# Graph layers of a GNN kernel: GpSimd waits for three landed gathers of the group in front before each group of four

## The reference

```python
def gcn_conv(x, W, b, src, dst, ew, num_nodes):
    h = x @ W
    deg = segment_sum(ew, dst, num_segments=num_nodes)
    dinv = where(deg > 0, rsqrt(deg), 0.0)
    norm = dinv[src] * ew * dinv[dst]
    agg = segment_sum(h[src] * norm[:, None], dst, num_segments=num_nodes)
    return agg + b
...
h = relu(batch_norm(gcn_conv(x, W1, b1, ...)))
h = relu(batch_norm(gcn_conv(h, W2, b2, ...)))
h = batch_norm(gcn_conv(h, W3, b3, ...))
out = layernorm(x + h)
```

## Time and profile before

| | us |
|---|---|
| three runs | 4579.43, 4584.94, 4593.61 |
| median | 4584.94 |
| profiled execution, its own time | 4592.19 |
| its span, first to last instruction | 4590.3 |
| busy: TensorE, VectorE, GpSimd, ScalarE | 2969.0, 2312.5, 2411.3, 1147.0 |
| mean granted TensorE clock, share of full | 0.823 |

### The profile page before, as it was taken

One profiled execution on the slowest core, in us unless ns is written; L12 is line 12 of the kernel. 1 busy time (PEld: TensorE's weight loads), 2 busy tenths in 40 slices (PEclk: granted clock), 3 DMA queues, 4 the chain that ended last, 5 costly groups with the idle time before them and its releaser, 6 DMA issues. The chain is left out here.

```text
span 4590.3 us, 52237 instructions
## 1 busy us (share of the span) xinstructions
PE 2969.0 (65%) x14449; PEld 2143.5 (47%) x14449; DVE 2312.5 (50%) x8186; ACT 1147.0 (25%) x2512; POOL 2411.3 (53%) x2514
## 2 busy tenths in 40 slices
PE   3895666666676666664420666777767776767774
PEld 3774656666666656663200433344433444433342
DVE  3774655655655555553522345533455534455435
ACT  1223556555655555552001200000000000000001
POOL 0002544444466666665577266665466664666662
PEclk9998778777787877776755889988899988999987
DMA  4896555565422322221000455555545545555552
GB/s 110 273 358 232 199 200 210 189 216 191 163 88 80 87 79 81 84 81 48 1 1 0 172 190 174 189 191 184 186 174 190 189 174 179 192 188 176 189 189 61
DMA packets 232026, 706.47 MB, mean 154 GB/s; under 512 B 62326, under 2 KB 111957, under 8 KB 212928
## 3 DMA queue, kind: packets, MB, share of 16 engines
q1 hardware_dynamic: 104252, 447.79, 26.7%
q0 software_dynamic: 93184, 191.21, 14.4%
q10 hardware_dynamic: 34308, 64.13, 4.3%
HBM read 559.66 MB, written 143.28 MB: 153 GB/s over the span
## 5 line engine op out<-in xcount | busy, mean ns | idle before, releaser
L552 POOL DMA_INDIRECT stage<-h_tab,earr x1248 | 1183.3, 948 | 810.8 <-issue 346.5
L527 POOL DMA_INDIRECT arena<-kv_tab,idxr x832 | 796.0, 957 | 970.3 <-ACT idxr L634 405.6
L1013 PE MATMUL bank<-arena,xr 128*128 128x512 f32 (+1 forms) x2058 | 1021.1, 638 | 5.6 <-issue 5.6
L992 PE MATMUL bank<-oh,stage 128*128 128x128 f32 x2496 | 394.3, 308 | 494.0 <-issue 487.8
L992 PEld LDWEIGHTS bank<-oh,stage 128*128 128x128 f32 x2496 | 354.1, 214 | 712.3 <-issue 701.1
L860 PE MATMUL bank<-xr,arena 128*128 x3328 | 494.0, 308 | 236.8 <-DVE arena L1254 146.9
L1572 DVE TENSOR_TENSOR sums<-sums,bank 128x128 f32 x1248 | 351.3, 282 | 568.3 <-remote 398.2
L1013 PEld LDWEIGHTS bank<-arena,xr 128*128 128x128 f32 x2058 | 407.6, 212 | 394.8 <-issue 394.8
L860 PEld LDWEIGHTS bank<-xr,arena 128*128 128x128 f32 x3328 | 456.0, 218 | 259.3 <-issue 258.2
L499 POOL DMA_INDIRECT a_tab<-tot,cell x416 | 416.0, 1000 | 261.2 <-DMA arena<-kv_tab,idxr 151.1
L709 ACT ACTIVATE rs<-mv,epsc 128x49 f32<-128x49 f32 (+1 forms) x6 | 1.9, 316 | 2003.3 <-DVE mv L1611 1692.6
(11 more groups left out here) (224 smaller groups left out, 2739.4 us busy)
## 6 DMA issues: line engine op xcount, KB each, us to landing
arena<-a_tab SPq DMA_DIRECT2D x147, 1792.0 KB
a_tab<-stage SPq DMA_DIRECT2D x49, 1792.0 KB
kv_tab<-stage SPq DMA_DIRECT2D x48, 768.0 KB, 8.5
arena<-key_d ACTq DMA_DIRECT2D x52, 512.0 KB, 7.1
arena<-ew_d ACTq DMA_DIRECT2D x52, 512.0 KB, 10.1
arena<-rel_d SPq DMA_DIRECT2D x52, 512.0 KB
stage<-h_tab,earr POOLq DMA_INDIRECT x1248
arena<-kv_tab,idxr POOLq DMA_INDIRECT x832
```

Source lines behind the costliest of these rows:

```text
L527: G.indirect_dma_start(kv[b % 3][:, t, :], None, kv_tab, bass.IndirectOffsetOnAxis(idxr[:, b % 3, t:t + 1], 0))\
L552: G.indirect_dma_start(gring[:, (q % NG) * GRP + s, :], None, h_tab[l], bass.IndirectOffsetOnAxis(src_i[:, t:t + 1], 0)).then_inc(row_land ...
L992: last = M.matmul(bank[q % NG][:, s * P:(s + 1) * P], gring[:, (q % NG) * GRP + s, :], oh[:, q % NG, s, :], start=True, stop=True)
L1013: mm = M.matmul(o_[:, 0:cw], xr[:, n, :], abuf[B % NBUF][:, n % KB, 0:cw], start=n == 0, stop=n == NT - 1)
```

## The change

Ahead of each group but the first of a layer, GpSimd now also waits until the first three gathers of the group in front have landed, and until the last gather of the group two in front has. For that the landings are told on other semaphores: the first three gathers of a group count on `row_land[q % 4]` (48 a group), the last one on one of two new semaphores `row_last[Q % 2]`. TensorE waits for both ahead of the group's sums.

```diff
+        row_last = [sem(f"row_last{a}") for a in range(2)]
...
                     Q = GQ * l + q
                     if Q >= NG:
                         pool.wait_ge(sum_done, Q - NG + 1)
+                    if q:
+                        pool.wait_ge(row_land[(q - 1) % NG], 48 * ((Q - 1) // NG + 1))
+                    if Q >= 2:
+                        pool.wait_ge(row_last[Q % 2], 16 * (Q // 2))
                     for s in range(GRP):
                         t = q * GRP + s
                         G.indirect_dma_start(gring[:, (q % NG) * GRP + s, :], None, h_tab[l],
-                                             bass.IndirectOffsetOnAxis(src_i[:, t:t + 1], 0)).then_inc(row_land[q % NG], 16)
+                                             bass.IndirectOffsetOnAxis(src_i[:, t:t + 1], 0))\
+                         .then_inc(row_land[q % NG] if s < GRP - 1 else row_last[Q % 2], 16)
...
             def sums(l, q):
                 Q = GQ * l + q
-                pe.wait_ge(row_land[q % NG], 64 * (Q // NG + 1))
+                pe.wait_ge(row_land[q % NG], 48 * (Q // NG + 1))
+                pe.wait_ge(row_last[Q % 2], 16 * (Q // 2 + 1))
```

## The result

The changed kernel takes 4943.9 us (median of 4 runs, 4942.1 to 4954.4) where the kernel before takes 4586.8 (4 runs): a ratio of 1.078, 95% interval 1.077 to 1.080, or 357 us more. The forecast was 4652, with a range up to 4750. The profiled execution has a span of 4940.2 us, against 4590.3 before.

The account below looks back on a forecast made before the run. It took GpSimd's stretch of gathers, with its stops for a full ring, to set each layer's time. 93 + 243 - 269 = +67 us on the median 4585 gave 4652 us, range 4530 to 4750.

Parts of the forecast that it names:

- Step (a): GpSimd's full-ring waits for sum_done ahead of groups go, except each layer's first: 269 us back.
- Step (b): New landing wait ahead of groups in quiet stretches: 0.30 us for each of 309 groups, 93 us (ends 0 and 155).
- Step (c): New landing wait beside block loads: 135 loads at 1.8 us, 243 us lost (ends 135 and 351).
- The rival built on that estimate: Landing wait hidden in quiet stretches, third gather back within 2.5 us: -26 us, 4559 us; chance 0.06.
- on the average half way: Beside block loads, each load meets one third gather, on the average half way: 1.8 us lost per load.
- The fast rival: Block loads fall in with the groups, next third gather meets only their end: -41 us, 4544 us; chance 0.24.
- Ring waits that stay in part: Quiet pauses too short for TensorE's news, half of the 269 us of ring waits stays: +202, 4787 us; chance 0.15.
- One for one: New pauses only stand where GpSimd's ring waits stood: no change, 4585 us; chance 0.09.
- +15 to +130: Whole kernel: range of the sum with the ends of (b) and (c) apart from each other, 4600 to 4715 us.

Follow-up runs that it names:

- second set: Follow-up runs on a chip where the kernel before took 4351.6 us: changed kernel with small loads or 768 KB loads, kernel before with the pause or half rows.
- small loads: Changed kernel, blocks behind the first four load 64 KB instead of 1,792 KB: ratio 1.048 in the second set, later 4606.4 us, 1.0036; kernel before likewise: 4563.7 us.
- the wait on the gather: Changed kernel with the landing wait written first, so the group's first gather carries it itself: 4791.0 us, ratio 1.049.
- timed pieces: Changed kernel, each block loaded in two pieces, each released by the landing of a group's third gather: 4659.6 us, ratio 1.0136.
- the pause: Kernel before plus four GpSimd memsets behind each group's wait for sum_done, no landing waited for: 1.056 in the second set, later 4629.2 us, 1.008.
- half rows: Kernel before, gathers behind the first four groups fetch 64 of 128 rows: ratio 0.995 in the second set, later 4600.8 us, 1.002.
- first, third and fourth set: Follow-up runs, each beside the kernel before, which took 4565.8, 4589.9 and 4591.1 us; the last two on one chip.

## Why the prediction was wrong, point by point

**Step (a), the ring waits: right in kind, 64 us too large.** The pauses for landings took the place of the waits for `sum_done`, as announced: "remote" is gone, the waits for TensorE are 60 us. 205 us came back and not 269. The step counted the 0.30 us of fixed gap ahead of the 113 stopping gathers as stop (290 is 256 without it), and assumed that only a layer's first full ring stays, 21 us, where 53 us net stay (9 of them at the first rings). Its reason, that the pauses together are long enough, held in the result and in three of the four sets; on the chip of the second set there is little to give back.

**Step (b), the quiet stretches: mis-sized, 0.72 instead of 0.30 us a group, 129 us too low.** The landing of a 64 KB gather comes 2.54 us behind its start (median of the small loads in the second set, whose trace has nearly all landings; the attention part's row has 3.00 with the restart in it), and the restart behind the landing takes 0.73 us and not 0.26, because the wait is an instruction of its own. In the earlier trace rows the instruction behind the landing, a scatter, carries its wait itself. The run with the wait on the gather shows 2.74 us from start to restart: for this form the step would have been right (0.27 measured, 0.30 forecast). The order of the instructions would have told it: in the changed kernel the gather carries `sum_done`, and the landing wait stands ahead by itself.

The Trainium skill has, in "DMA: Bandwidth & Descriptors", section "Anatomy of one DMA — SWDGE (gpsimd) path", a price of about 2.0 us plus the bytes over 436 GB/s; for 64 KB that is an estimate of 2.15 us. The traces do not agree, they have 2.54. The rival built on that estimate fell: with the better of the two restarts 2.15 + 0.26 = 2.41 us would have been hidden, and 2.74 were measured.

**Step (c), the loads: mis-sized, 2.5 instead of 1.8 us, 88 us too low.** The number of loads and the mechanism are right: with small loads 342 us go. The step that failed is "on the average half way". Loads don't meet the groups at random. In the timeline above the load is issued at 3707.11 and the third gather starts at 3708.08, close to the worst place. 75 of 139 loads stand like that and cost 3.8 us each, 41 stand about 1 us behind a third gather's start and cost 0.9 us, so they bunch in two places. That they do so because each load follows TensorE's dense steps, once its news is prompt, fits the rows but wasn't tested by itself. The fast rival had seen that the loads would fall into step, and put all of them behind the third landing. The timed pieces show that at that place the price is 0.28 us: the rival's mechanism is real, but most loads were not there.

**The other rivals.** Ring waits that stay in part: 53 us of them, not 135. Its reason, quiet pauses too short for the news, is seen in the run with small loads, where 57 us of "remote" stay; the loads' long stops are what cleared them in the changed kernel. One for one: right for stops that meet no load (+17 us with small loads, +39 for the pause), which is what a chip with late news gives; the loads made the rest.

The range ended at 4750, below the 4822 that the upper ends of (b) and (c) give together (155 + 351 - 269 = +237); it took for granted that both don't fall high at once, and both did, (b) beyond its end. The narrower +15 to +130 doesn't follow from the ends either: with one of the two terms at its end the sum already runs from -41 to +175. With the measured 222, 331 and 205 it is 4585 + 222 + 331 - 205 = 4933, within 11 us of the result.

## What to carry to other kernels

A wait that looks free because another wait disappears has to be priced in its own form: see which of several waits the instruction itself carries, and take the restart from a row of that form. A new wait for a landing couples the gathers to whatever else uses the DMA engines: work out at which point of the group the large transfer starts, and don't average. If a stop can't be explained by work, run the kernel on another chip before building on it.

## What the hardware showed that I had not expected

TensorE's posts reach GpSimd, VectorE and SyncE late in some traces and not in others. In the result and in the first, third and fourth set they were late, on two chips at least; in the second set, all on a third chip, they were prompt, and the kernel before is 5% faster (4352 us). That it is the chip fits this, but no chip was seen in both ways. In the late traces a layer's gathers take 600 to 609 us in the kernel before (with small loads and half rows too); the stretch seen in the second set is 534 us (with half the rows, a kernel 21 us faster than B). Not all of the 5% lies there: of the 277 us between the two runs with half rows, 176 are in the gathers' stretches and 87 ahead of the first of them, in a part that this change doesn't touch. Where news is late, it goes by gathers issued, 1.44 to 1.46 us each, not by their rows (128 or 64) and not by the size of the loads beside them (1,792 or 64 KB).

What is held up there isn't settled: no view shows the post on its way. One rival stands untested, the recording of the trace itself. Where news is late, the trace lacks records: 278 of 312 posts of `sum_done` and 15% of the gathers' landings are there in the kernel before, and 56% of the landings in the changed kernel. In the second set all posts are there, and 99% of the landings in the run with half rows. No run here tells whether the recording causes the delay or only suffers from the same thing.

GpSimd starts again 0.26 us behind a landing that the next gather waits for itself, and 0.73 us behind one that a wait instruction of its own takes.

A gather issued as a load of 1,792 KB starts lands when the load has drained: 7.22 us from start to restart against 3.32 in quiet. Two pieces of the same block, started behind a third gather's landing, cost 0.28 us together.
